# Two programs of a fused transformer kernel made one: keys, values and ternary weights with the first feed-forward

## The reference, cut to what matters

```python
# first feed-forward: rows and weights quantised
scale_x = 127 / clip(max|x|, 1e-5);  x_dq = clip(round(x * scale_x), -128, 127) / scale_x
gamma_w = clip(mean|w|, 1e-5);       w_dq = clip(round(w / gamma_w), -1, 1) * gamma_w
gate = silu(x_dq @ gate_w.T + gate_b);  val = x_dq @ val_w.T + val_b
out = bit_linear(gate * val, out_w, out_b)      # quantises its own input in the same way
# second attention, its keys and values from the context
k = rmsnorm(ctx @ Wk + bk) * kn_w;   v = ctx @ Wv + bv
```

## Time and profile before

| | |
|---|---|
| median of 3 runs | 1779.12 us (1778.63 to 1782.15) |
| the profiled execution, its own time | 1780.04 us |
| its span in the trace | 1778.1 us |
| TensorE busy | 1707.0 us (96% of the span) |
| VectorE busy | 1242.4 us (70%) |
| ScalarE busy | 924.0 us (52%) |
| GpSimd busy | 594.6 us (33%) |
| mean granted TensorE clock | 0.991 of full speed |

### The profile page before, as it was taken

How to read it: one execution, slowest core, us unless ns; L and a number is a source line. 1 busy time by engine, 2 the same in 40 slices (tenths; PEclk the granted TensorE clock), 3 DMA queues, 4 the chain that set the end, 5 groups by cost and what they waited for, 6 DMA issues and landing times. The chain is left out here.

```text
span 1778.1 us, 26445 instructions
## 1 busy us (share of the span) xinstructions
PE 1707.0 (96%) x9562; PEld 1392.2 (78%) x9582; DVE 1242.4 (70%) x2313; ACT 924.0 (52%) x1774; POOL 594.6 (33%) x469
## 2 busy tenths in 40 slices
PE   7999998997999979999999999999899999999998
PEld 6998997774444458888788788878777799999876
DVE  5444443786888768888788788888768567767555
ACT  4443342564566466666666666666331365656411
POOL 3111143233677632221222212121210255555342
PEclk9999999998999999999999999999999999999999
DMA  9323210854143572121232222110161579797573
GB/s 319 93 86 103 76 49 4 305 207 136 36 95 75 149 234 92 61 84 60 89 104 88 87 63 84 60 60 1 49 252 59 190 247 306 256 305 251 191 245 108
DMA packets 175564, 238.25 MB, mean 134 GB/s; under 512 B 51270, under 2 KB 112454, under 8 KB 173254
## 3 DMA queue, kind: packets, MB, share of 16 engines
q1 hardware_dynamic: 156620, 203.14, 35.0%
q0 software_dynamic: 9600, 33.30, 6.0%
q10 hardware_dynamic: 9216, 0.14, 0.3%
HBM read 184.24 MB, written 43.78 MB: 128 GB/s over the span
## 5 line engine op out<-in xcount | busy, mean ns | idle before, releaser
L1233 POOL TENSOR_TENSOR a_rq<-a_ssq,a_qhalf 128x4 f32<-128x4 f32 x64 | 66.1, 1033 | 358.9 <-DMA a_ssq<-a_sum_row 358.9
L78 PE MATMUL bank<-a_xT_hi,a_wq_lo 128*128 128x512 f32 (+1 forms) x384 | 144.5, 376 | 1.4 <-DVE a_xT_lo L503 1.4
L80 PE MATMUL bank<-a_xT_hi,a_wq_hi 128*128 128x512 f32 (+1 forms) x384 | 139.0, 362 | 0.0
L79 PE MATMUL bank<-a_xT_lo,a_wq_hi 128*128 128x512 f32 (+1 forms) x384 | 138.4, 361 | 0.0
L78 PE MATMUL bank<-a_wo_hi,a_oT_lo 128*128 128x512 f32 x320 | 127.4, 398 | 5.9 <-POOL a_wo_lo L1246 4.1
L1396 ACT ACTIVATE a_scores<-a_scores,a_nmax 128x256 f32<-128x256 f32 x256 | 126.9, 512 | 0.8 <-DVE a_nmax L1573 0.8
L80 PE MATMUL bank<-a_wo_hi,a_oT_hi 128*128 128x512 f32 x320 | 125.7, 393 | 0.0
L79 PE MATMUL bank<-a_wo_lo,a_oT_hi 128*128 128x512 f32 x320 | 125.7, 393 | 0.0
L2123 POOL TENSOR_TENSOR e_wg_lo<-raw_g,e_wg_hi 128x1408 fp32r<-128x1408 f32 x25 | 87.9, 3516 | 112.3 <-ACT e_wg_hi L2195 112.3
L1385 ACT ACTIVATE a_sum_row<-bank,a_sum_eps 1x512 f32<-1x512 f32 x64 | 43.3, 677 | 142.3 <-PE bank L1765 142.3
L1273 POOL TENSOR_TENSOR f_h<-f_vv,f_gs 128x512 f32<-128x512 f32 x64 | 92.7, 1452 | 60.4 <-DVE f_vv L1503 59.7
(11 more groups left out here) (423 smaller groups left out, 5403.1 us busy)
## 6 DMA issues: line engine op xcount, KB each, us to landing
raw_g<-in_egw SPq DMA_DIRECT2D x26, 704.0 KB, 4.8
raw_u<-in_euw SPq DMA_DIRECT2D x26, 704.0 KB, 6.2
a_xT_hi<-x1T_hi SPq DMA_DIRECT2D x16, 1024.0 KB, 6.1
a_xT_lo<-x1T_lo SPq DMA_DIRECT2D x16, 1024.0 KB, 8.2
raw_d<-in_edw SPq DMA_DIRECT2D x26, 512.0 KB, 5.8
y_routed<-m_y SPq DMA_DIRECT2D x39, 256.0 KB, 6.7
raw_d<-in_edw SPq DMA_DIRECT2D x26, 192.0 KB, 6.7
a_cTraw<-in_ctxT SPq DMA_DIRECT2D x8, 512.0 KB, 5.8
```

Of the source, the lines that this page charges most:

```text
L78: pe.matmul(out, w[1], x[0], start=first, stop=False)
L79: pe.matmul(out, w[0], x[1], start=False, stop=False)
L80: return pe.matmul(out, w[0], x[0], start=False, stop=last)
L1233: pool.tensor_tensor(rq[:, h % HG, :], ssq[u % 2][:], qhalf[:], ALU.pow).then_inc(s_rq, 1)
```

## The change

The keys, values and ternary weights no longer are a program of their own: `keys_values_ternary` returns its parts of each engine's list, and `ffn0_attention1` puts them ahead of its own in one program. Semaphores take the place of the meeting. Lines that only changed their indentation are left out:

```diff
-        kb, ktb, vb = banks[0:2], banks[2:4], banks[4:6]
+    kb, vb, ktb = banks[0:2], banks[2:4], banks[4:6]
...
             for j in range(3):
-                pool.memset(prep.rT[j][:], 0.0)
+            pool.memset(prep.rT[j][:], 0.0).then_inc(s_rT0, 1)
...
                     scaled(0)
+            if t == T - 2:
             round_x(0)
             round_x(1)
-            keys_out(T - 2)
-            keys_out(T - 1)
+        return keys_out
...
                     values_out(t - 1)
+            if t == T - 1:
+                quantised_x(0)
+                quantised_x(1)
                 summed(t)
...
                     largest()
-                if t == T - 2:
                     scales()
-            quantised_x(0)
-            quantised_x(1)
             values_out(T - 1)
...
-            for t in range(T - 1):
+        for t in range(T):
                 keys(t)
...
                     transposed(t - 2)
-                if t < T - 2:
                     values(t)
-            keys(T - 1)
-            transposed(T - 3)
-            values(T - 2)
-            values(T - 1)
-            transposed(T - 2)
-            transposed(T - 1)
+        return transposed
...
+            kv.sync(sp)
             sp.dma_start(ahead.raw[:], wq_dram[:, :, 0:D]).then_inc(s_raw, 16)
-            sp.dma_start(first.mask[:], mask_dram).then_inc(s_raw, 16)
-            sp.dma_start(first.bq[:], bq_dram).then_inc(s_raw, 16)
             for s, count in zip(stored, (B // 2, B // 2 - 1, 1)):
                 sp.wait_ge(s, count * 32)
+            sp.dma_start(first.mask[:], mask_dram).then_inc(s_raw, 16)
+            sp.dma_start(first.bq[:], bq_dram).then_inc(s_raw, 16)
...
         def _(pool):
+            kv.gpsimd(pool)
+            pool.wait_ge(kv.normed, T)
+            pool.wait_ge(kv.values, T)
...
-            round_x(2)
+            keys_out = kv.scalar(act)
+            act.wait_ge(kv.cleared, 3)
             xT_copy(0)
+            round_x(2)
+            keys_out(T - 2)
             xT_copy(1)
+            keys_out(T - 1)
             round_x(3)
...
-            for t in range(*GROUPS[1]):
-                norm(t)
+            kv.vector(dve)
             quantised_x(2)
-            quantised_x(3)
+            dve.wait_ge(kv.biases, 32)
             for n in range(T):
...
                 val(n, 0)
+                if n == 0:
+                    norm(GT)
+                    norm(GT + 1)
...
                 val(n, 1)
+                if n == 0:
+                    norm(GT + 2)
+                    norm(GT + 3)
...
                 val(n, 2)
+                if n == 0:
+                    quantised_x(3)
...
+            keys_transposed = kv.tensor(pe)
+            pe.wait_ge(kv.quantised, 2)
             x_transposed(0)
+            keys_transposed(T - 2)
             x_transposed(1)
+            pe.wait_ge(kv.ternary, len(W) * keep.chunks)
+            pe.wait_ge(kv.keys, T)
+            pe.wait_ge(kv.values, T)
             for n in range(T):
                 up(n, range(1))
+                if n == 0:
+                    keys_transposed(T - 1)
+                    pe.wait_ge(kv.staged, T)
```

More of the change, by code:

```diff
@@ new lines, in sem @@
+    def sem(name):
+        return ctx.semaphore("kv_" + name)
+    mem = Region(nc, keep.base)
+    kst, vst = mem.take("kv_kst", [P, 2, G, S]), mem.take("kv_vst", [P, 2, QT, D])
+    kf = [mem.take(f"kv_kf{j}", [P, G, HD]) for j in range(2)]
+    ksq = [mem.take(f"kv_ksq{j}", [P, G, HD]) for j in range(2)]
+    bk = mem.take("kv_bk", [P, D])
+    assert mem.offset <= keep.area
+    mem = Region(nc, keep.area)
+    ring = [mem.take(f"kv_ring{j}", [P, CH]) for j in range(RING)]
+    assert mem.offset <= keep.high
@@ new lines, in keys_values_ternary @@
+    mem = Region(nc, kv.end)
+    cTraw = [ahead.ctx, mem.take("kv_cTraw", [P, KD, S])]
+    wk, wv, cT = kv.wk, kv.wv, kv.cT
+    sb = lambda name, shape: mem.take("kv_" + name, shape)
+    bv = sb("bv", [P, D])
+    qn, kn, wn, eps_rms = (sb(n, [P, 1]) for n in ("qn", "kn", "wn", "eps_rms"))
+    ksum, krms, rk = (sb(n, [P, T, G]) for n in ("ksum", "krms", "rk"))
+    stats, std = sb("stats", [P, QT, 6]), sb("std", [P, T])
+    assert mem.offset <= keep.limit
+    mv, magic, rgamma = keep.mv, keep.magic, keep.rgamma
@@ new lines, in keys_values_ternary @@
+    s_ring = [sem(f"ring{j}_loaded") for j in range(RING)]
+    s_sc, s_min, s_done = sem("scaled"), sem("min"), sem("ternary")
+    s_stats, s_mv, s_std, s_rstd = sem("stats"), sem("mean_var"), sem("std"), sem("rstd")
+    s_bias, s_xn, s_ax, s_qx, s_sx, s_sg, s_rg, s_rp, s_xr = (sem(n) for n in (
+        "next_biases_loaded", "next_xn", "next_absmax", "next_step", "next_scale", "next_scales", "next_rscale",
+        "next_rscale_parts", "next_rounded"))
+    s_xq, s_rT0 = sem("next_quantised"), sem("next_rT_cleared")
@@ new lines, in tensor, with keys, transposed, values @@
+    def tensor(pe):
+        def keys(t):
+            after(pe, s_clo, t + 1 - READY)
+            after(pe, s_kf, max(t - 1, 0))
+            for k in range(KD):
+                last = matmul3(pe, kb[t % 2][:], part(cT[t % 3], slice(None), k), part(wk, slice(None), k), k == 0,
+                               k == KD - 1)
+            last.then_inc(s_k, 1)
+        def transposed(t):
+            pe.wait_ge(s_kn, t + 1)
+            after(pe, s_kev, max(t - 1, 0))
+            for g in range(G):
+                last = pe.transpose(ktb[t % 2][:, g * P:(g + 1) * P], ksq[t % 2][:, g, :], ident[:])
+            last.then_inc(s_kt, 1)
+        def values(t):
+            after(pe, s_vf, max(t - 1, 0))
+            for k in range(KD):
+                last = matmul3(pe, vb[t % 2][:], part(cT[t % 3], slice(None), k), part(wv, slice(None), k), k == 0,
+                               k == KD - 1)
+            last.then_inc(s_v, 1)
+        for t in range(T):
+            keys(t)
+            if t >= 2:
+                transposed(t - 2)
+            values(t)
+        return transposed
```

490 lines of the change are left out of this document (219 added, 271 removed).

## The result

The changed kernel took 1783.65 us, the median of 14 executions (1780.39 to 1786.62), beside 1779.88 for the kernel before (14 executions, 1778.59 to 1784.12): a ratio of 1.0018, 95% interval 1.001 to 1.0025. The forecast was 1779.2 us in a range up to 1781.3.

What follows compares the result with a forecast made beforehand. Tile 0's row scale was taken to bound the kernel: 3.66 us won less 1.36 (keys transposes 15, staging), 0.96 (normalisations), 0.40 (conversion) and 1.01 (port) gave -0.07, so 1779.12 became 1779.2 us, range 1776.2 to 1781.3.

Steps and rivals of the forecast that it cites:

- What bounds the kernel: Around 419 to 451 us, x tile 0's row scale, behind GpSimd's fourth product, sets when TensorE gets on; `round_h(0)` at 436.10.
- The last tiles and the gate: Last key tiles to first copy, which waits for GpSimd's clears: x tile 1's transposes start at 417.13, 3.66 us won.
- Given back on TensorE and ScalarE: Keys transposes 15 and staging ahead of quarter 1 give back 1.36 us, leaving 2.30; first silu 0.22 us later.
- Given back on VectorE: Between `val` 1 and 3: two normalisations 0.96 us, a conversion 0.40, one port delay 1.01.
- the port: Lock shared by VectorE and GpSimd, behind `val` 1: one delay of 1.01 us taken, bounds 0 and 2.02.
- Everything behind keeps its time: GpSimd's fourth product ends at 434.3, as good as before, so all later work is unchanged.
- a fall of the clock: Rival: TensorE's clock stays low through quarter 1 of tile 0, 1.5 us on top, 1780.7 us; chance 0.12.
- The whole gain: Rival: TensorE's 3.66 us won at the start reach the end, 1775.5 us; chance 0.09.
- The miss at the port: Rival: VectorE's normalisations and GpSimd's products miss each other behind `val` 1, 0.94 us stay, 1778.2 us; chance 0.25.

Runs made afterwards that it cites:

- silu first: Changed kernel with the wait for staged keys moved to the first `down` and `keys_out(15)` behind the first silu: 1779.36 us, ratio 0.9997.
- warm pair: Kernel before and the joined kernel in the old order, both with extra products in tiles 1 and 2 and attention0's last turn: 1777.78 and 1776.26 us.
- second pair: Second traces of the kernel before and the changed kernel, both run once more unaltered: medians 1778.99 and 1783.03 us.
- first pair: First traces of the kernel before and the changed kernel, from the original measurement: medians 1779.88 and 1783.65 us.
- warm kernels: Kernel before and changed kernel, both with extra products in tiles 1 and 2 and attention0's last turn: 1777.78 and 1779.91 us.
- the join alone: One joined program with every engine's list in the order of the kernel before, semaphores in place of the meeting: 1780.59 us, ratio 0.9999.

## Why the prediction was wrong

**What bounds the kernel: right.** `round_h(0)` decides when tile 1 and tile 2 run; the time from `round_h(0)` to `round_h(1)` is between 12.04 and 12.16 us in all sixteen traces.

**The last tiles and the gate: right, the gain a little too small.** I had 3.66 us won at x tile 1's transposes, and 4.1 came. `keys_out(13)` started at 411.42 + 2.25 = 413.67 instead of 413.97, so the conversions hid more than I took, and the clears, with the store ahead of them, ended 1.5 us behind that staging (413.60 for 412.09) instead of 1.69.

**Given back on TensorE and ScalarE: right in kind.** 2.3 us forecast for quarter 1, 2.8 measured. The first silu came 0.3 us earlier instead of 0.2 later. It was held by the table, as said, and undoing that (silu first) is worth 1.1 us at `round_h(0)`.

**Given back on VectorE: the port was the term mis-sized.** I took one delay of 1.01 us, with two, 2.02, as the bound. Both normalisations were stopped: 2.95 us for the pair against the 0.97 of the free one, 1.98 us of delay. The bound was in the text, the mean was in the sum. By the Trainium skill's page "SBUF — State Buffer" (section "Who interferes with whom") the loser is blocked for a whole instruction of the other; the trace agrees: the normalisations took 1.54 and 1.49 us instead of about 0.5 beside products of 1.27 and 1.44, so each lost about one. I had argued that one product falls ahead of one normalisation; but a second product was ready, since its silu followed the first at once. The sum by measured terms is -2.8 + 3.0 + 0.34 (conversion) = +0.6 us, which is the 0.6 us of `round_h(0)`. In the second traces it was 128.53 - 127.62 = 0.9; two traces of one kernel differ by 0.3 to 0.7 us here. That `round_h(0)` came so near to 436.1 is partly luck: the port cost 1 us more than I took, and quarter 1 came 0.5 us earlier.

**"Everything behind keeps its time": wrong, and the step that failed.** I had let a fall of the clock in as a rival, at 1.5 us and 0.12, but in quarter 1 of tile 0, and argued against it with the 1.8 us stop in tile 2 that left the clock at 1.00. That was one execution. The second trace of the same kernel shows the same stops and 0.54 from 450 to 453. In both of the changed kernel's traces the fall was there, in tile 2, at 1.7 and 1.5 us. A second part of the same step I had not named at all: the end of the joined program. The meeting behind it took 0.6 us longer in all eleven traces, and the products behind that meeting 1.3 us longer in the warm pair and 0.9 in the second pair, at the low clock (in the first pair 0.6 shorter).

**The range** reached to 1781.3 because port and clock had been kept apart as cases, each small. They came together: with the 2.1 us that stayed in the warm kernels (1.3 of them in tile 0 by the traces, the rest at the next meeting) and 1.7 for the clock, 1779.12 + 2.1 + 1.7 is 1782.9, beside a measured 1783.65. And the chance of 0.06 for slower by more than 0.2% (3.6 us) was too low; the median is at 0.18% by ratio, right at that bound.

**The other rivals.** The whole gain didn't pass through; with the join alone it nearly does up to the first query (3.0 of 3.66 us), where the four normalisations and the conversion stay in idle time. The miss at the port didn't happen in any of the six traces with the late normalisations: the stops add up to about 2 us in each, as one double one or two single ones.

## What to carry to other kernels

A meeting of the engines is also a place where prepared work lies in idle time; if a join moves that work behind the first products, see what runs on the engine that shares the port, and take the bound where a queue of its instructions is ready, not the mean. Look also at the next meeting: what the joined program saved at one, it may in part pay there. Before a 0.2% change is costed from one trace, ask of every stop near the critical path whether TensorE's clock falls there in some executions: a second trace of the unaltered kernel tells it. Here the order of the kernel before, joined, with a few extra products gave 1776.3 us (ratio 0.9983), and the changed order with the normalisations early and extra products in tiles 1 and 2 gave 1775.9 (0.998); both lie below the two kernels, by about 0.2%.

## What the runs showed of the hardware that I had not expected

TensorE can fall to its lower level after stops far shorter than those at the boundary: 1.8 and 0.9 us within tile 2, 1.2, 1.4 and 1.3 us in attention0's last turn, and it stayed low for about 3 us of work. Whether it falls differs between executions of one kernel with the same stops. The Trainium skill (page "TensorE: Matmul & The Clock Gate", section "Part 1: The HAM clock gate (the "warmup" mystery)") says that the gate watches activity on a clock of its own, which doesn't start with the kernel; that would fit, but no run here shows the gate. And where it falls matters more than that it falls: at 435 to 441 us and at 525 to 531 it cost nothing, at 450 us 1.5 to 1.7, in attention0 2.1 to 2.4. Eighteen products that nothing reads (nine in each of tiles 1 and 2) took 2.5 us off the changed kernel's median.
